# A ternary feed-forward kernel: order of the first stage, and the layout of x and out

## What is computed

```python
w = weights[conditions]
c = jnp.einsum('bct,bcd->bdt', x, w)

def ternarize(W, threshold):                 # threshold = 0.05
    absW = jnp.abs(W)
    delta = threshold * jnp.max(absW)
    mask = absW > delta
    n = jnp.maximum(jnp.sum(mask), 1)
    alpha = jnp.sum(jnp.where(mask, absW, 0.0)) / n
    return alpha * jnp.sign(W) * mask

h = jax.nn.gelu(c @ ternarize(W1).T + b1, approximate=False)   # W1: 2048 x 512
y = h @ ternarize(W2).T + b2                                   # W2: 512 x 2048
scale = jnp.max(jnp.abs(y)) / 7 + 1e-8
out = x + jnp.clip(jnp.round(y / scale), -7, 7) * scale
```

## Time and profile before

| | us |
|---|---|
| median of 3 runs | 1028.4 (1027.22 to 1029.46) |
| the profiled execution | 1038.57 |
| its span | 1036.8 |

### The profile page before, as it was taken

How to read it: one execution, slowest core, us unless ns; L and a number is a source line. 1 busy time by engine, 2 the same in 40 slices (tenths; PEclk the granted TensorE clock), 3 DMA queues, 4 the chain that set the end, 5 groups by cost and what they waited for, 6 DMA issues and landing times.

```text
span 1036.8 us, 14562 instructions
## 1 busy us (share of the span) xinstructions
PE 937.0 (90%) x5088; PEld 440.7 (43%) x5088; DVE 648.6 (63%) x1025; ACT 544.4 (53%) x688; POOL 148.3 (14%) x187
## 2 busy tenths in 40 slices
PE   2779999999999999999999999999999999999600
PEld 2344444444444444444444444444444444444200
DVE  7796756566665666566666665665665665633492
ACT  5576553638273654637282745536372635635290
POOL 3510002030303011030303020020303020000000
PEclk9899999999999999999999999999999999999955
DMA  8400112112031112121030111121120211105999
GB/s 340 135 5 0 41 43 50 41 36 55 10 67 24 40 44 47 40 51 40 10 81 10 40 47 44 42 49 40 27 64 10 44 45 43 41 0 183 304 385 382
DMA packets 39421, 77.85 MB, mean 75 GB/s; under 512 B 3952, under 2 KB 4080, under 8 KB 38896
## 3 DMA queue, kind: packets, MB, share of 16 engines
q1 hardware_dynamic: 35136, 73.41, 24.2%
q0 software_dynamic: 3840, 3.94, 1.4%
q10 hardware_dynamic: 432, 0.34, 0.1%
HBM read 60.89 MB, written 16.78 MB: 75 GB/s over the span
## 4 chain that ended last, share of the span: by engine, by line
PE 49%; issue 20%; DVE 11%; DMA 9%; ACT 4%; POOL 2%; another core or an unknown queue 1%; SPq 1%; DVEq 0%; POOLq 0%; ACTq 0%
PE ps L421 22%; PE ps L431 21%; DMA yx<-in_x 6%; PE ps L484 3%; PE ps L401 3%; DVE st L692 2%; POOL wg L339 2%; DVE wts L725 2%; DMA wg<-in_L_cond_weights,ids 1%; DMA y<-in_L_ffn_W 1%; ACT y L675 1%; ACT g L548 1%; DVE st L871 1%; ACT ws L570 1%
## 5 line engine op out<-in xcount | busy, mean ns | idle before, releaser
L421 PE MATMUL ps<-yc,wts 128*128 128x512 f16 x2048 | 450.5, 381 | 13.0 <-ACT g L582 7.0
L431 PE MATMUL ps<-wts 128*128 128x512 f16 x1792 | 391.4, 379 | 0.0
L421 PEld LDWEIGHTS ps<-yc,wts 128*128 128x128 f16 x2048 | 199.8, 98 | 260.1 <-ACT g L582 12.8
L725 DVE SCALAR_TENSOR_TENSOR wts<-g,st,wts 128x512 f16<-128x512 f32 x256 | 186.5, 750 | 119.6 <-ACT wts L587 118.0
L431 PEld LDWEIGHTS ps<-wts 128*128 128x128 f16 x1792 | 173.5, 98 | 204.8
L582 ACT ACTIVATE g<-ps,b1t,st 128x512 f32<-128x512 f32 x256 | 197.8, 773 | 116.3 <-PE ps L421 98.0
L587 ACT ACTIVATE wts<-g,st 128x512 f16<-128x512 f32 x256 | 181.1, 714 | 0.0
L569 ACT ACTIVATE xs<-yx,st 128x2048 f16<-128x2048 f32 x28 | 56.1, 2002 | 176.3 <-DVE st L759 167.3
L355 POOL PARTITION_ALL_REDUCE st<-st x46 | 21.9, 478 | 696.6 <-DVE st L694 404.9
L339 POOL DMA_INDIRECT wg<-in_L_cond_weights,ids x112 | 110.9, 990 | 41.5 <-issue 30.9
L730 DVE SCALAR_TENSOR_TENSOR y<-ps,st,b2b 128x512 f32 (+1 forms) x56 | 41.7, 749 | 90.0 <-PE ps L431 75.1
(11 more groups left out here) (127 smaller groups left out, 368.8 us busy)
## 6 DMA issues: line engine op xcount, KB each, us to landing
yx<-in_x SPq DMA_DIRECT2D x56, 512.0 KB, 6.1
out<-wts SPq DMA_DIRECT2D x12, 512.0 KB, 10.1
wts<-in_x SPq DMA_DIRECT2D x10, 512.0 KB, 6.1
wts<-in_x SPq DMA_DIRECT2D x4, 1024.0 KB, 5.6
y<-in_L_ffn_W SPq DMA_DIRECT2D x8, 512.0 KB, 11.0
y<-in_L_ffn_W SPq DMA_DIRECT2D x4, 1024.0 KB, 17.8
y<-in_x SPq DMA_DIRECT2D x4, 1024.0 KB, 11.5
out<-y SPq DMA_DIRECT2D x4, 1024.0 KB, 12.5
```

The lines of the kernel that those rows point to most:

```text
L421: last = nc.tensor.matmul(psH[:, j % HB, :], T1T[:, j // HC, k, j % HC * P:(j % HC + 1) * P], csp[:, a, k, :], start=(k == 0 and a == 0), ...
L431: last = nc.tensor.matmul(psY[:, r % 2, :], hsp[:, a, j, r * P:(r + 1) * P], T2T[:, j, :], start=(j == 0 and a == 0), stop=(j == HT - 1 an ...
L725: nc.vector.scalar_tensor_tensor(out=hsp[:, 1, j, :], in0=g[:, j % HB, :], scalar=s_h, in1=hsp[:, 0, j, :], op0=ALU.mult, op1=ALU.subtract ...
```

## The change

1. TensorE counts all four quarters of W1's mask right behind C of block 0, ahead of the hidden tiles. The count goes to `psN1`, the fourth hidden bank, and so hidden tile 3 waits for `n_read`.
2. VectorE makes masks 1 to 3 ahead of ternary quarter 0 and of the low halves of C; ternary quarter 1 goes behind the scales. The low halves of h, the ternary quarters and the maxima of W2 are interleaved in another way: twelve low halves instead of ten stand ahead of the first ternary quarter of W2, four between it and the second.
3. `count2` of all quarters moves to j = 12 of the product with W2, with the wait for the copy of C.
4. `spread_w` of block 1 moves behind the gelu of tile 3 on ScalarE; the maximum of b1 moves behind the first maximum of W1 on VectorE.
5. x and out are passed to the kernel as [32, 2, 64, 2, 512] (half block, batch parity, row, tile, column), rearranged outside. One partition's two rows of a half block lie side by side, 4 KB. `load_half` takes two such pieces to a partition instead of four rows. The four batches of a half block now lie in SBUF in the order 0, 2, 1, 3, which `condition` follows.

```diff
-    x_v = x.rearrange("b c t -> (b c) t").rearrange("(n p) t -> p n t", p=P)
-    x_cbt = x.rearrange("b c t -> c b t")
-    out_v = out.rearrange("b c t -> (b c) t").rearrange("(n p) t -> p n t", p=P)
+    x_v = x.rearrange("g s c n t -> (s c) g n t")
+    x_cgs = x.rearrange("g s c n t -> c g s (n t)")
+    out_v = out.rearrange("g s c n t -> (s c) g n t")
...
-        psN = ps[:, HB, :]
+        psN1, psN2 = psH[:, HB - 1, :], ps[:, HB, :]
...
                 for a in range(2):
-                    sp.dma_start(xd[a * C:(a + 1) * C, :, :], x_cbt[:, bass.ds(first_batch, HALF), :])\
+                    sp.dma_start(xd[a * C:(a + 1) * C, :, :].rearrange("p (s n) t -> p s (n t)", s=2),
+                                 x_cgs[:, bass.ds(half_block, 1), :, :].rearrange("c g s t -> c (g s) t"))\
                         .then_inc(xd_loaded, 16)
...
-            def rows_of(view, rows, n):
-                return view[:, rows, :].rearrange("p (m n) t -> p m n t", n=n.stop - n.start)
+            def rows_of(view, halves, n):
+                return view[:, halves, n, :]
...
                         n = half * HALF + j
+                        at = half * HALF + j % 2 * 2 + j // 2
                         for a in range(2):
-                            last = nc.tensor.matmul(psC[:, k, j * C:(j + 1) * C], xs[:, n, tk], ws[:, a, n, :],
+                            last = nc.tensor.matmul(psC[:, k, j * C:(j + 1) * C], xs[:, at, tk], ws[:, a, n, :],
...
             condition_direct(0, 1, psC0)
+            for c in range(WCH):
+                count1(c)
 
             pe.wait_ge(c0_split, 2)
-            COUNTS = {0: (0, 1), 1: (2,), 2: (3,)}
             for j in range(HT):
                 pe.wait_ge(t1_made, j // HC + 1)
+                if j == HB - 1:
+                    pe.wait_ge(n_read, 1)
                 first(0, j, wait_bank=j >= HB, wait_c=False)
-                for c in COUNTS.get(j, ()):
-                    count1(c)
-
-            pe.wait_ge(n_read, 1)
+
             pe.wait_ge(xdirect_loaded[1], 16)
...
-            pe.wait_ge(c_copied, 1)
             pe.wait_ge(g_made, HT)
             for j in range(HT):
                 if j % HC == 0:
                     pe.wait_ge(t2_made, j // HC + 1)
-                    count2(j // HC)
+                if j == 3 * HC:
+                    pe.wait_ge(c_copied, 1)
+                    for c in range(WCH):
+                        count2(c)
...
-            pe.wait_ge(c_copied, 2)
...
-            spread_w(1)
             act.wait_ge(relu_summed, WCH)
-            hidden(0, lambda j: None, wait_c=False)
+            hidden(0, lambda j: spread_w(1) if j == 3 else None, wait_c=False)
...
+            for c in range(1, WCH):
+                mask_w1(c)
             ternary1(0)
             dve.wait_ge(cscale_ready, 1)
             low_c0(0, psC)
             low_c0(1, psC0)
-            for c in range(1, WCH):
-                mask_w1(c)
-            ternary1(1)
             dve.wait_ge(relu_summed, WCH)
...
+            ternary1(1)
+            low_h(0, 0)
             ternary1(2)
-            low_h(0, 0)
+            low_h(0, 1)
+            low_h(0, 2)
+            max_w2(0)
+            low_h(0, 3)
+            low_h(0, 4)
             ternary1(3)
-            low_h(0, 1)
-            for c in range(WCH):
+            for c in range(1, WCH):
+                low_h(0, 2 * c + 3)
+                low_h(0, 2 * c + 4)
                 last = max_w2(c)
-                low_h(0, 2 * c + 2)
-                if c < WCH - 1:
-                    low_h(0, 2 * c + 3)
...
-            low_h(0, 9)
+            low_h(0, 11)
...
             ternary2(0)
-            for j in range(10, 14):
+            for j in range(12, HT):
                 low_h(0, j)
             ternary2(1)
-            for j in range(14, HT):
-                low_h(0, j)
             max_c(1, link)
```

More of the change, by code:

```diff
@@ L18, in build @@
 def build(nc, x, cond, wcond, W1, b1, W2, b2, out):
-    B, C, T = x.shape
+    HALVES, _, C, _, T = x.shape
+    B = cond.shape[0]
     S = wcond.shape[0]
@@ L254, in load_direct, with load_half @@
             def load_direct(b):
-                sp.dma_start(xdirect[b], x_v[:, b * RT:(b + 1) * RT, :]).then_inc(xdirect_loaded[b], 16)
-            def load_half(n, first_batch):
+                sp.dma_start(xdirect[b].rearrange("p (m n) t -> p m n t", m=2), x_v[:, 2 * b:2 * b + 2, :, :]).then_inc(xdirect_loaded[b], 16)
+            def load_half(n, half_block):
                 for a in range(2):
-                    sp.dma_start(xd[a * C:(a + 1) * C, :, :], x_cbt[:, bass.ds(first_batch, HALF), :])\
+                    sp.dma_start(xd[a * C:(a + 1) * C, :, :].rearrange("p (s n) t -> p s (n t)", s=2),
+                                 x_cgs[:, bass.ds(half_block, 1), :, :].rearrange("c g s t -> c (g s) t"))\
                         .then_inc(xd_loaded, 16)
@@ L272, in _ @@
             load_direct(1)
-            load_half(0, DIRECT * BB)
+            load_half(0, 2 * DIRECT)
             with sp.Fori(1, 2 * (NB - DIRECT)) as n:
                 sp.wait_ge(x_split, n)
-                load_half(n, n * HALF + DIRECT * BB)
+                load_half(n, n + 2 * DIRECT)
             def transfers(b, m, n):
                 cut = [slice(i, i + 1) for i in range(m.start, m.stop)] if b in APART else [m]
-                return [(slice(b * RT + 2 * c.start + n.start, b * RT + 2 * (c.stop - 1) + n.stop), x_piece(b, c, n), n) for c in cut]
-            def rows_of(view, rows, n):
-                return view[:, rows, :].rearrange("p (m n) t -> p m n t", n=n.stop - n.start)
+                return [(slice(2 * b + c.start, 2 * b + c.stop), x_piece(b, c, n), n) for c in cut]
+            def rows_of(view, halves, n):
+                return view[:, halves, n, :]
             def load_tail(b):
@@ L291, in load_half_tail @@
                 m = slice(h, h + 1)
-                sp.dma_start(x_piece(b, m, ALL), rows_of(x_v, slice(b * RT + 2 * h, b * RT + 2 * h + 2), ALL))\
+                sp.dma_start(x_piece(b, m, ALL), rows_of(x_v, slice(2 * b + h, 2 * b + h + 1), ALL))\
                     .then_inc(xt_half_loaded[b][h], 16)
@@ L441, in count1 @@
                 for n in range(WCH):
-                    last = nc.tensor.matmul(psN, twos[:, :], quarter(mask1, c, n), start=(c == 0 and n == 0),
+                    last = nc.tensor.matmul(psN1, twos[:, :], quarter(mask1, c, n), start=(c == 0 and n == 0),
                                             stop=(c == WCH - 1 and n == WCH - 1))
@@ L448, in count2 @@
                 for n in range(WCH):
-                    last = nc.tensor.matmul(psN, twos[:, :], quarter(neg2, c, n), start=(c == 0 and n == 0),
+                    last = nc.tensor.matmul(psN2, twos[:, :], quarter(neg2, c, n), start=(c == 0 and n == 0),
                                             stop=(c == WCH - 1 and n == WCH - 1))
@@ L803, in _ @@
             nc.vector.memset(twos[:, :], 2.0).then_inc(consts_made, 1)
-            dve.wait_ge(b1_loaded, 16)
-            nc.vector.tensor_reduce(xwb[:, 2:3], b1t[:, :], AX.X, ALU.max, apply_absolute_value=True)
             dve.wait_ge(xdirect_loaded[0], 16)
@@ L816, in _ @@
                 last = max_w1(c)
+                if c == 0:
+                    dve.wait_ge(b1_loaded, 16)
+                    nc.vector.tensor_reduce(xwb[:, 2:3], b1t[:, :], AX.X, ALU.max, apply_absolute_value=True)
             link(last)
@@ L857, in _ @@
             dve.wait_ge(n1_counted, 1)
-            nc.vector.tensor_reduce(n1, psN, AX.X, ALU.add).then_inc(n_read, 1)
+            nc.vector.tensor_reduce(n1, psN1, AX.X, ALU.add).then_inc(n_read, 1)
             dve.wait_ge(n_read, 1)
@@ L913, in _ @@
             dve.wait_ge(n2_counted, 1)
-            nc.vector.tensor_reduce(n2n, psN, AX.X, ALU.add).then_inc(n2_read, 1)
+            nc.vector.tensor_reduce(n2n, psN2, AX.X, ALU.add).then_inc(n2_read, 1)
             dve.wait_ge(n2_read, 1)
@@ L1034 @@
         a = inputs[name]
-        if name == "L0_ffn_W1":
+        if name == "x":
+            a = _np.reshape(a, (32, 2, 2, 64, 512)).transpose(0, 2, 3, 1, 4)
+        elif name == "L0_ffn_W1":
             a = _np.reshape(a, (4, 512, 4, 128)).transpose(3, 0, 2, 1)
@@ L1046 @@
     r = _run(nc, [arrays], core_ids=[0])
-    return r.results[0]["out_0"]
+    return _np.reshape(r.results[0]["out_0"], (32, 2, 64, 2, 512)).transpose(0, 3, 1, 2, 4).reshape(128, 64, 512)
```

## The result

The changed kernel takes **1013.6 us** (median of 4 runs, 1013.1 to 1013.86) where before takes 1028.6; the ratio is 0.9855 (95% interval 0.9838 to 0.9872), so 15.0 us off. I had said 1015.6, with 12.8 off. A ratio is taken over the single runs of both kernels, so it need not be the quotient of the two medians given.

A forecast was written before the change was run, and what follows sets the result against it. TensorE was taken to bound the body and transfers the tail. The next product 12.8 earlier, with 0 for the layout, gave 1015.6 of the median; range 1008.5 to 1020.5, leaving out some 2 in 10.

The forecast's parts named there:

- (1): First stage: masks and counts of W1 first put the scale at 35.9, 8.0 earlier; first hidden product 3.6 later.
- (2): VectorE from scale to first ternary quarter of W2: 27.9, plus 2.5 lost on the first low half, ending at 66.3.
- (3): TensorE's path through block 1's hidden rows, two at half clock (3.2): second product starts at 67.2, bounds 65.0 and 69.5.
- (4): Counts of W2 behind three quarters of the second product: 31.1 together, next product at 98.3, 12.8 earlier; quarter four's margin 0.5.
- (5): Spread of block 1's weights behind the fourth gelu: 0.8 on ScalarE, which has slack; GpSimd's later gather hidden, margin 2.5.
- (6): Layout of x and out, 2 KB runs to 4 KB: taken as 0; the cited page's rule would give 1.7.
- rival A: Transfers gain too: body loads up to 0.9 faster, tail smoother; 3 to 8.6 beyond the sum, 1007 to 1012.6; chance 0.17.
- gelu waits vanish: Sign of rival A: TensorE's waits on gelu behind 140 us, 7.0 us in 8 waits, gone from the changed profile.
- the dip in the tail: Transfers in the tail falling to 189 GB/s over 3 us; worth 1.6 if it went, counted in rival A.
- Rival B: A new wait (W2's quarter four, the gather or the clock) eats part: 3 to 8 less gain, 1018.5 to 1023.5; chance 0.16.
- C: Slower: 4 KB runs over 64 partitions clash and lengthen the body loads; 1031 or more; chance 0.04.
- D: Nothing arrives: TensorE loses at the second product what it won; 1027 to 1030; chance 0.03.

The follow-up runs named there:

- Experiment 6: The changed kernel with the masks and counts of W1 back in the order of before; 1028.74 us beside 1038.67 for before, ratio 0.9908.
- Experiment 7: The changed kernel with 16 filling matmuls on TensorE behind the counts of W1; 1020.44 us beside 1038.67 for before, ratio 0.984.
- Experiment 5: The changed kernel with the counts of W2 and the wait for the copy of C back in their places; 1026.45 us beside 1038.67 for before, ratio 0.9886.
- experiment 8: The changed kernel with the spread of block 1's weights back in front of the first gelu; 1024.49 us beside 1038.67 for before, ratio 0.9869.
- experiment 2: The kernel before with only the layout of x and out changed; 1027.1 us against 1028.34 for before, ratio 0.9983.
- experiment 3: The changed kernel with the layout of x and out undone, so only the first stage changed; 1015.47 us, ratio 0.9871 to before.
- experiment 11: The changed kernel with the stores back in 2 KB runs; 1015.81 us against 1013.28 for the changed kernel, ratio 0.9875 to before.
- experiment 4: The changed kernel with the body's half-block loads back in 2 KB runs, tail loads and stores still 4 KB; 1012.98 us, ratio 0.9846 to before.
- experiment 1: The kernel before, unchanged, profiled once more; that execution took 1027.25 us.
- experiment 10: The changed kernel with GpSimd's maximum of the first half block put between the fourth and fifth gather; 1013.25 us, ratio 0.9852 to before.

## Why the prediction was right, and where it was not

- **(1) The scale.** Said 35.9, with the first tile at 32.7. Measured: reduce at 32.59, its chain's last step at 35.34, tile at 32.67. Right. Experiment 6 prices the step and what hangs on it at 6.2 us in the start of the second product and 7.9 in the next one's, about 6 in the ratio.
- **(2) VectorE's path.** Said 66.3 after a wait of 2.5 for the first low half. It waited 1.44 and ended at 65.1. The working was right, the wait too large.
- **(3) TensorE's path.** Said 67.2, the later of the two; it was 65.36, and TensorE's path indeed ended last (no idle time in front of L491), by 0.3. The term that was mis-sized is the clock's: I had taken two whole tiles at half clock, 3.2 us, where the earlier trace rows show one (two at its 3.59 would even have been 3.7); the 128 matmuls took 29.28 instead of 27.8, so it cost 1.5. It is no fixed price: in the other traces with these hidden tiles unchanged they took 29.1 to 30.4. Experiment 7 took away just this, and the start moved by 1.5, to 63.86. That is below my lower bound, 65.0, which I had called that of the full clock though my own sum for it was 64.0.
- **(4) The counts of W2 moved.** Said: 31.1 for the product, clock kept, quarter four in time by 0.5. Measured 31.1 (65.36 to 96.44), clock 1.00, in time by 0.7. Experiment 5 prices the move at 3.5 us of start; the other 1.0 of its delay is the clock of the hidden tiles.
- **(5) The spread.** I called it 0.8 us beside other work, with nothing gained by the move, and this missed the point of it. In its old place it waits for a gather (6.1 us in before's trace, in the view of the earlier trace rows but not among my rows), and the gelus are queued behind that wait. Before, the count was later than the gather, so it cost nothing there; once the scale came early it would have cost 2.4 (experiment 8). My sum for the changed kernel was not hurt, since it had the spread in its new place. GpSimd's queue was as said: gathers from 44.45, the maximum of W2 at 60.3, no wait.
- **(6) The layout.** Said 0, measured 1.9 (experiments 2 and 3). This is the step that failed. I had set the W1 loads (4 KB runs, 400 GB/s) against stores and loads in 2 KB runs (409, 405) and found no difference, but the W1 loads ran beside gathers and other streams and are no clean rate of 4 KB runs. In like stretches of one stage it is 408 against 420 (experiment 11), 2.9%. The page I had cited, the Trainium skill's DMA: Bandwidth & Descriptors ("Why small descriptors are slow"), names two costs of a small piece: 3 cycles for each packet, from which I had estimated 2.2%, and 32 bytes of metadata with each DMA operation, which I had left out. With both the estimate is 3.0%, and the stores agree (2.9%). Its rule had the sign right, where my rows had not; but 0.8 of the 1.7 us that I had worked out from it lay in the body loads, and that these gain nothing was right (experiment 4). A stretch of before's own trace that I had not read, with W2 coming in, 8 KB to a partition, was a hint (columns as in the earlier trace rows):

```profile
20.00:22.00 2.00, 2.00 (x11) 2.00 (x11) 1.51 (x5) 0.89 (x1) 0.64 (x2) 1.00 1.01 422
```

- **The wrong witness.** I said the gelu waits behind 140 us would stay near 7 us. They were gone, and rival A had leaned on them. They belonged to the profiled execution, whose 10 us over the median I had noted and not asked about: 9 of them are the body (864.2 against 855.1). So "gelu waits vanish", my sign for A, came up without A.
- **The sum.** 12.8 forecast for the first stage, 12.9 measured (experiment 3), with a start that was 12.2 earlier than in experiment 1's execution of before (108.59 to 96.44), 14.1 than in experiment 2's (110.51) and 14.6 than in the first. The start of before moves by 2.5 between executions, so the close agreement of the first-stage sum is partly luck: I put the changed kernel's next product at 98.3, 1.9 later than it came, and took before's from an execution in which it was 0.5 to 2.5 later than in the two others, and these two misses cancel. Of A only a faster tail came, 1.9 us, some 1.1 of it the stores (experiment 11); the body loads did not gain, and the dip in the tail, which was to be worth 1.6, is still there (199 GB/s from 960 to 963 us, before 189). Rival B did not occur, nor C or D.

## What to carry to other kernels

In a start that waits for a scalar made from all the data, put the work that the scalar needs in front even if the first product starts later, and then look at what else stands in front of the consumers: here a copy that waited for a gather was harmless only as long as the scalar was late. Move whatever reads a shared bank out of the way of the product, so that the engine never idles in front of it. And when a profiled execution is longer than the median of the runs, find out where, before any of its waits becomes a term or a rival.

## What the hardware showed that I had not expected

- The same kernel took 1028.3 and 1029.4 us on two chips and 1038.7 on a third (medians of 15, 9 and 9 runs). In the five traces with the stop VectorE stands 2.0 to 2.9 us in 5 to 8 of 13 turns, always at the y store that it reaches as GpSimd's eighth gather starts, and it goes on 1.1 us behind the start of GpSimd's maximum (1.8 to 1.9 in three of the 35 stops). The trace names no engine as the releaser. Whether GpSimd holds it was not settled (experiment 10 ran on a chip without the stop).
- At full DMA share, stores moved 408 GB/s in runs of 2 KB and 420 in runs of 4 KB (24 us of the tail each), while loads to 64 partitions landed in 6.0 to 6.2 us in the former and 6.2 to 6.3 in the latter.
- Idle time of TensorE of 3.6 us ahead of the hidden tiles (and of 2.65 in experiment 6) was followed by a clock of 0.50; idle time of 3.5 us in experiment 5 was not. In the first stage of before, one and the same gap of 2.3 us was followed by the lower clock in two executions (the first, and experiment 2's, where that stage is unchanged) and not in experiment 1's. What a gap costs is not fixed by its length.
